# Attention denominators: a fifth accumulating DMA joins two partial sums, and TensorE runs two denominator groups for each unit instead of three

## The reference, cut to what matters

```python
q = (x @ Wq.T).reshape(b, t, h_kv, g, d).transpose(0, 2, 3, 1, 4)
k = (x @ Wk.T).reshape(b, t, h_kv, d).transpose(0, 2, 1, 3)
v = (x @ Wv.T).reshape(b, t, h_kv, d).transpose(0, 2, 1, 3)
att = jnp.einsum('bhgqd,bhkd->bhgqk', q, k) / scale
att = jax.nn.softmax(att, axis=-1)
y = jnp.einsum('bhgqk,bhkd->bhgqd', att, v)
```

## Time and profile before

| what | before |
|---|---|
| median of 3 runs | 3620.88 us (3619.24 to 3621.19) |
| the profiled execution, its own time | 3621.32 us |
| its span | 3619.7 us |
| PE busy | 3493.0 us, 96% of the span |
| DVE busy | 2232.6 us, 62% |
| ACT busy | 1593.6 us, 44% |
| POOL busy | 1602.2 us, 44% |
| mean busy share of the DMA engines over the attention stage | about 55% |

### The profile page before, as it was taken

One profiled execution on the slowest core, in us unless ns is written; L12 is line 12 of the kernel. 1 busy time (PEld: TensorE's weight loads), 2 busy tenths in 40 slices (PEclk: granted clock), 3 DMA queues, 4 the chain that ended last, 5 costly groups with the idle time before them and its releaser, 6 DMA issues. The chain is left out here.

```text
span 3619.7 us, 46130 instructions
## 1 busy us (share of the span) xinstructions
PE 3493.0 (96%) x17196; PEld 2320.7 (64%) x17196; DVE 2232.6 (62%) x3725; ACT 1593.6 (44%) x2990; POOL 1602.2 (44%) x700
## 2 busy tenths in 40 slices
PE   6999899999999999999999889799999999999999
PEld 4778455555555555555555268688888888887787
DVE  5541877777777777777777178544444444442627
ACT  3210266666666666666666533222222222213544
POOL 1111288898889989898899800000000000000010
PEclk8999699999999999999999989899999999999999
DMA  6662455656555555555554444711111111113222
GB/s 226 204 186 82 114 118 103 124 107 120 108 109 119 112 113 112 120 109 118 108 108 93 96 151 172 204 30 29 29 30 29 29 30 29 29 41 117 90 66 85
DMA packets 196074, 361.96 MB, mean 100 GB/s; under 512 B 41728, under 2 KB 122880, under 8 KB 175680
## 3 DMA queue, kind: packets, MB, share of 16 engines
q0 software_dynamic: 37104, 202.92, 24.7%
q1 hardware_dynamic: 156496, 154.69, 15.6%
q10 hardware_dynamic: 2304, 2.10, 0.2%
HBM read 162.13 MB, written 62.78 MB: 62 GB/s over the span
## 5 line engine op out<-in xcount | busy, mean ns | idle before, releaser
L772 DVE TENSOR_REDUCE att_chunk_max<-att_scores 128x1 f32<-128x512 f32 x2048 | 1268.9, 683 | 349.7 <-PE att_scores L843 347.5
L753 ACT ACTIVATE att_exp<-att_scores_T 128x512 f32<-128x512 f32 x2048 | 1042.7, 603 | 507.4 <-PE att_scores_T L857 503.4
L697 POOL TENSOR_TENSOR att_exp_pair<-att_exp 128x2048 f32<-128x2048 f32 x256 | 1198.6, 4727 | 133.1 <-ACT att_exp L753 132.8
L843 PE MATMUL att_scores<-att_k_stack,att_q_stack 96*128 96x512 f32 x2048 | 875.8, 450 | 16.7 <-DMA att_q_stack<-q_scratch 12.9
L857 PE MATMUL att_scores_T<-att_q_stack,att_k_stack 98*128 98x512 f32 x2048 | 745.3, 402 | 3.3 <-ACT att_exp L753 3.2
L843 PEld LDWEIGHTS att_scores<-att_k_stack,att_q_stack 96*128 96x128 f32 x2048 | 392.1, 192 | 427.2 <-DVE att_chunk_max L772 267.9
L868 PE MATMUL att_y_acc<-att_exp,att_v_head 128*32 128x512 f32 x4096 | 494.4, 600 | 0.0
L857 PEld LDWEIGHTS att_scores_T<-att_q_stack,att_k_stack 98*128 98x128 f32 x2048 | 386.4, 189 | 148.4 <-ACT att_exp L753 63.5
L1229 POOL DMA_DIRECT2D inter_scratch<-gu_inter x84 | 45.2, 538 | 884.6 <-DVE gu_inter L1172 884.6
L1283 ACT ACTIVATE gu_magnitude<-gu_value 128x512 f32<-128x512 f32 x88 | 55.7, 633 | 516.7 <-DVE gu_value L1314 516.7
L1313 DVE TENSOR_TENSOR gu_rounded<-gu_up_acc,gu_rounded 128x512 f32<-128x512 f32 x88 | 60.9, 692 | 323.7 <-PE gu_up_acc L1348 323.7
(11 more groups left out here) (191 smaller groups left out, 4925.1 us busy)
## 6 DMA issues: line engine op xcount, KB each, us to landing
att_exp_pair<-att_exp_pair POOLq DMA_DIRECT2D x128, 1024.0 KB, 7.2
att_q_stack<-q_scratch SPq DMA_DIRECT2D x96, 256.0 KB, 5.7
shared_raw<-in_wd_t POOLq DMA_DIRECT2D x34, 256.0 KB, 3.5
qkv_x_tile<-in_x SPq DMA_DIRECT2D x16, 512.0 KB, 4.8
q_scratch<-qkv_qk_out_hi POOLq DMA_DIRECT2D x32, 256.0 KB, 3.1
q_scratch<-qkv_qk_out_lo POOLq DMA_DIRECT2D x32, 256.0 KB, 4.3
qkv_wqkv_raw<-in_wmod POOLq DMA_DIRECT2D x8, 1024.0 KB, 7.4
qkv_wmod<-in_wmod POOLq DMA_DIRECT2D x8, 1024.0 KB, 8.2
```

Of the source, the lines that this page charges most:

```text
L697: nc.gpsimd.tensor_tensor(ps[PAIR_SLOT[j]][:], pr[2 * j % NP][:], pr[(2 * j + 1) % NP][:], ALU.add).then_inc(pair_done, 1)
L753: nc.scalar.activation(pr[k % NP][:, h * NB:(h + 1) * NB], stp[bank(u, c, GH * k + h)][:], ACT.Exp, scale=INV_SQRT_DH).then_inc(exp_done, 1)
L772: nc.vector.reduce_max(cmax[c % 2][:, q:q + 1], turn_buffer(u, c, q)[:], AX.X).then_inc(sm_done, steps_done(u, q))
L843: nc.tensor.matmul(turn_buffer(u, c, q)[:], qs[c % 4][0:SR, h, qt * P:(qt + 1) * P], ks[c // QB % 2][0:SR, kc * NB:(kc + 1) * NB], start=T ...
```

## The change

A fifth accumulating DMA (sum 4) adds slot 3 (pairs 6 and 7) to slot 4 (pairs 4 and 5). It is issued by GpSimd in the next unit, between pair 0 and pair 1, and it waits for sum 3 and the quad sum of the unit before. TensorE then has two denominator groups instead of three, at k = 0 and k = 8 of the next unit; the copy of the denominators moves from k = 6 to k = 8, and the reciprocal from k = 9 to k = 11. Pair 3 now waits for sum 4 of the unit before, where it waited for a denominator group. In the last unit sums 3 and 4 are not made: TensorE takes slots 0, 4, 3 and 2 in four groups.

```diff
--- before.py
+++ after.py
@@ -467,16 +467,17 @@
     NP, NS = 8, 5
     PAIRS = KT // 2
     PAIR_SLOT = (0, 1, 2, 3, 4, 1, 3, 2)
-    DMA_SUM = ((0, 1), (2, 3), (0, 2), (3, 2))
-    SUM_PAIRS = (1, 3, 3, 7)
+    DMA_SUM = ((0, 1), (2, 3), (0, 2), (3, 2), (4, 3))
+    SUM_PAIRS = (1, 3, 3, 7, 7)
     DMA_AFTER = {1: 0, 3: 1, 4: 2, 7: 3}
     QUAD_AFTER = 5
-    DEN_SLOT = (0, 4, 3)
+    DEN_SLOT = (0, 4)
     ND = len(DEN_SLOT)
-    DEN_AT = (0, 2, 6)
+    DEN_AT = (0, 8)
+    LAST_SLOT = (0, 4, 3, 2)
     RP = 8
-    DEN_COPY = 6
-    RECIP_AT = 9
+    DEN_COPY = 8
+    RECIP_AT = 11
     Y_AFTER = 5
     DW = GH * NB // P
     TSTEP = 14
@@ -685,7 +686,8 @@
                     if u:
                         pool.wait_ge(dma_sum[3], u * 16)
                 elif j == 3:
-                    pool.wait_ge(den_done, 3 + u * ND)
+                    if u:
+                        pool.wait_ge(dma_sum[4], u * 16)
                 elif j == 4:
                     pool.wait_ge(den_done, 2 + u * ND)
                 elif j == 5:
@@ -703,6 +705,9 @@
                 if i == 2:
                     pool.wait_ge(dma_sum[0], 16 + u * 16)
                     pool.wait_ge(dma_sum[1], 16 + u * 16)
+                elif i == 4:
+                    pool.wait_ge(dma_sum[3], 16 + u * 16)
+                    pool.wait_ge(quad_done, u + 1)
                 pool.dma_start(ps[into][:], ps[other][:], accum_op=ALU.add).then_inc(dma_sum[i], 16)
 
             def quad_sum(u):
@@ -718,8 +723,10 @@
 
             def unit(u, c, g):
                 for j in range(PAIRS):
+                    if j == 1 and not is_first(u):
+                        sum_by_dma(u - 1, 4)
                     pair(u, j)
-                    if j in DMA_AFTER:
+                    if j in DMA_AFTER and not (beyond(u, 1) and j == PAIRS - 1):
                         sum_by_dma(u, DMA_AFTER[j])
                     if j == QUAD_AFTER:
                         quad_sum(u)
@@ -869,20 +876,34 @@
                                            pr[k % NP][:, h * NB:(h + 1) * NB], start=(k == 0), stop=(k == KT - 1))
                 ins.then_inc(pv_done, 1)
 
+            def ones_by(slot, first, last):
+
+                part = ps[slot]
+                for h in range(GH):
+                    ins = nc.tensor.matmul(dp[h * DH:(h + 1) * DH, :], ones[:], part[:, h * NB:(h + 1) * NB],
+                                           start=first, stop=last)
+                return ins
+
             def denominators(u, i):
 
                 if i == 0:
                     pe.wait_ge(dma_sum[2], 16 + u * 16)
                     pe.wait_ge(den_copied, u + 1)
-                elif i == 1:
-                    pe.wait_ge(quad_done, u + 1)
                 else:
-                    pe.wait_ge(dma_sum[3], 16 + u * 16)
-                part = ps[DEN_SLOT[i]]
-                for h in range(GH):
-                    ins = nc.tensor.matmul(dp[h * DH:(h + 1) * DH, :], ones[:], part[:, h * NB:(h + 1) * NB],
-                                           start=(i == 0), stop=(i == ND - 1))
-                ins.then_inc(den_done, 1)
+                    pe.wait_ge(dma_sum[4], 16 + u * 16)
+                ones_by(DEN_SLOT[i], i == 0, i == ND - 1).then_inc(den_done, 1)
+
+            def last_denominators(u):
+
+                pe.wait_ge(dma_sum[2], 16 + u * 16)
+                pe.wait_ge(den_copied, u + 1)
+                pe.wait_ge(quad_done, u + 1)
+                ones_by(LAST_SLOT[0], True, False)
+                ones_by(LAST_SLOT[1], False, False)
+                pe.wait_ge(pair_done, NP // 2 + 7 + u * PAIRS)
+                ones_by(LAST_SLOT[2], False, False)
+                pe.wait_ge(pair_done, NP // 2 + 8 + u * PAIRS)
+                ones_by(LAST_SLOT[3], False, True).then_inc(den_done, ND)
 
             def unit(u, c, g):
                 for k in range(KT):
@@ -931,8 +952,7 @@
             units(pe, unit)
             for b in (2, 1):
                 by_v(NU - 1, (NU - 1) % BODY, HKV - 1, KT - b)
-            for i in range(ND):
-                denominators(NU - 1, i)
+            last_denominators(NU - 1)
 
 
 def stage_out_projection(nc, ctx, x, y_dram, bo, mod_dram, x1_dram, wo_raw, h2_hi, h2lo_dram, modT, ident,
```

## The result

The changed kernel takes 3652.57 us (median of 4 runs, 3650.47 to 3654.25); the kernel before took 3620.06 us beside it. The ratio is 1.009, with a 95% interval of 1.0072 to 1.0107. I forecast 3673, slower by 52 us; it is slower by 32.5. The direction, the engine that bounds and the range held. The size came out 20 us too high.

The account below looks back on a forecast made before the run. TensorE bounds the kernel before; GpSimd would bound the changed one, the unit going from 51.70 to 53.57 us. 56.1 (30 units) + 3.5 (last unit) - 7.3 (end) = +52.3 on 3621.3: 3673.6, median 3673; range 3648 to 3710.

Parts of the forecast that it names:

- What bounds the kernel now: In attention before the change: TensorE sets the pace, busy 399.04 of 400 us, with GpSimd close behind at 354.75.
- The slack: GpSimd's waits for exponentials before the change, 42.3 us over 1200 us: 1.82 us a unit, counted as free.
- 12.15: GpSimd's stretch from sum 0 to sum 1 before the change: two pairs, 10.33 us, plus 1.82 waiting for exponentials.
- The new wait and issue: On GpSimd between sum 3 and sum 0: 13.82 us where 10.33 stood, 2.5 of it waiting and 0.9 issue.
- TensorE's saving: One denominator group fewer on TensorE: 0.87 us a unit, 27 us over 31 units if only this counted.
- The stretch from sum 1 to sum 2: On GpSimd: pair 4, then a wait until sum 1 has landed; taken as 8.65 us, as before the change.
- The end: End of attention: the reciprocal starts about 2.0 us after pair 7 instead of 9.28, a gain of 7.3 us.
- the last stretch: From sum 3 of unit 30 to the end of pair 7: 49.43 us before, 3.5 more after the change.
- TensorE would wait 2.7 us at k = 8 for sum 4: At the denominator group on k = 8, TensorE waits some 2.7 us a unit, without reaching GpSimd.
- The slower-clock rival: TensorE falls to its slower clock through its waits at k = 8: +120 us, 3741; 7 in 100.
- The faster rival: Sum 3 lands behind pair 0, so no wait: 3603, or 3587 if sum 1 lands as fast; 4 in 100.

## Why the forecast held, and where it was off

- *What bounds the kernel now: TensorE, with GpSimd 1.82 us a unit behind it.* Right on the engine, and shown from both sides: a group more costs 0.86 us a unit, and a wait of 2.0 us on GpSimd costs 0.5. The slack was read 0.3 too large. Part of the waiting for exponentials stands ahead of pair 4, as the 0.33 at 1016.87 in the earlier trace rows; there sum 1 is already in flight, and GpSimd must wait for its landing next in any case. Over units 1 to 30 this part is 0.29 us a unit, so the slack was 1.5, and 2.0 less 1.5 is the 0.5 measured. My sum compared whole cycles and did not use the 1.82, but placing all of it between sums 0 and 1 (12.15, where 11.88 was measured) is why the stretches added up to 51.92.
- *The new wait and issue, 3.49 us a unit on GpSimd.* Right: 8.02 + 5.82 in place of 10.42 is 3.42.
- *TensorE's saving is worth nothing.* Right; a group put back costs nothing either.
- *The stretch from sum 1 to sum 2, 8.65 "on average", carried over from before.* This is the term that was mis-sized: 7.73. The landing of a sum was taken as a property of the sum, but 0.86 us of it was the company of another queue's loads, which the change itself moved. I had looked at that trip (the reciprocal, two tiles later) only for what waits for it, and costed it at nothing. It was worth -27 us; the whole cycle of the forecast, 53.57 against 52.72, was 25.5 us too long over 30 units. Two of my own numbers could have shown it: sum 1 at 7.8 and more in nearly every unit, the other sums at 7.0 to 7.1 in most.
- *The end, -7.3.* Right: -7.2 in the trace, -7.9 measured alone. Two small terms fell short by 3 us between them: sum 3 of unit 0 came 1.7 later, which I had at nothing, and the last stretch took 4.9 more instead of 3.5.
- *TensorE would wait 2.7 us at k = 8 for sum 4.* Wrong in its place. TensorE's idle time is there, 1.2 us a unit (391.11 of 400 us busy), but it arises at k = 0, where it waits for the row maxima (the later of their two stores lands in 3.2 us at the median, where it was 1.9); at k = 8 sum 4 has landed in most units. It changed nothing, since GpSimd doesn't wait for either.
- *The slower-clock rival.* It did not decide. Granted clocks of 0.97 to 0.99 stand in stretches of the changed kernel where 1.00 stood, but they are paid from TensorE's spare time.
- *The faster rival* needed a landing in 5.3 us. The shortest landing of sum 3 was 6.9.

The Trainium skill ("DMA: Bandwidth & Descriptors", section "Queues, rings and completion order") says that a DMA engine takes turns between its queues at packet granularity, and finishes a whole packet of one before it takes the next. No trace here shows packets or turns, so this case can't decide that rule. What the traces show is the outcome. The store of the reciprocal landed within 1.4 us when SP issued it 0.48 us behind sum 1 (1016.15 to SP's next step at 1017.58). Issued 4.7 us into sum 1, it landed after 3.2 us, 0.6 us behind the sum.

## What to carry to other kernels

An engine's slack is only its waits for other engines; its waits for its own transfers are work, and so is a wait for another engine that is spent while such a transfer is in flight and must be waited for next. So a transfer that the issuing engine must see land before its next step belongs where the list holds enough other work to cover the landing: two pairs apart instead of one, the same five sums turned 32 us of loss into 19 us of gain (8 of the 19 come from the last unit's groups). "Enough" is measured by the longest landing, not the mean: two pairs covered 10 us, not the 11.6 to 13.1 of every fourth unit. And a landing time read from a trace belongs to its neighbours in time as much as to the transfer: where a change moves another queue's DMAs, ask whose flight they leave and whose they enter, and whether anybody waits for those.

## What the runs showed of the hardware that I had not expected

- Four 64 KB loads of another queue inside the flight of a 1 MB SBUF to SBUF sum lengthen its landing by 0.7 to 0.9 us (8.03 against 7.17; 7.91 against 7.25), and in the cycles shown the issue of the four takes 4.05 us instead of 1.98.
- An 8 KB store issued into the middle of such a sum lands in 3 to 4 us at the median instead of 1.4 to 1.9. It seems to be held until the sum has landed: 30 stores of the reciprocal in the changed kernel, issued 0.6 to 5.4 us into a sum, all landed 0.2 to 0.8 us behind it.
- Seven 256 KB loads issued just ahead of such a sum lengthen its landing to 11.6 to 13.1 us.
- Behind a landing, a pair sum on GpSimd starts 0.07 us later, a DMA's issue 0.53 to 0.56 us later.
